# Moving the choose product from VectorE to GpSimd, and all block totals to ScalarE, in a graph network's edge ranking

## The reference, cut to what matters

```
src = concat([s, d, loop]); dst = concat([d, s, loop])      # 206250 edges, sorted by dst
x = layernorm(x + attention(x, src, dst))                    # softmax over the edges of a node
x = layernorm(x + edge_network(x, src, dst))                 # two batch norms over edges
x = layernorm(x + graph_convolution(x, src, dst))
x = layernorm(x + weighted_sum_mlp(x, src, dst, edge_weight))
```

## Time and profile before

| | us |
|---|---|
| median of 3 runs | 10757.82 (10753.19 to 10758.09) |
| the profiled execution | 10751.21 |
| its span | 10749.4 |
| VectorE busy | 8209.4 (76%) |
| TensorE busy | 8389.9 (78%) |
| ScalarE busy | 4510.4 (42%) |
| GpSimd busy | 1386.4 (13%) |

### The profile page before, as it was taken

How to read it: one execution, slowest core, us unless ns; L and a number is a source line. 1 busy time by engine, 2 the same in 40 slices (tenths; PEclk the granted TensorE clock), 3 DMA queues, 4 the chain that set the end, 5 groups by cost and what they waited for, 6 DMA issues and landing times. The chain is left out here.

```text
span 10749.4 us, 313973 instructions
## 1 busy us (share of the span) xinstructions
PE 8389.9 (78%) x96214; PEld 6815.6 (63%) x96215; DVE 8209.4 (76%) x16705; ACT 4510.4 (42%) x9074; POOL 1386.4 (13%) x1678
## 2 busy tenths in 40 slices
PE   2244668885888755899995999798999959769996
PEld 0232225664777644899994666444999936468896
DVE  4797777777999866666666999777888777788887
ACT  0120001113666411565654444586777746423333
POOL 0110001110000000466662000000000012100000
PEclk7555555556999855999997999899999979889998
DMA  2000000001444311333331888686455400000000
GB/s 49 4 0 13 4 4 11 12 12 47 162 161 161 124 36 36 109 122 125 122 125 58 273 275 274 227 291 210 143 144 145 139 12 5 4 4 3 3 3 13
DMA packets 618663, 984.99 MB, mean 92 GB/s; under 512 B 133030, under 2 KB 278381, under 8 KB 618586
## 3 DMA queue, kind: packets, MB, share of 16 engines
q1 hardware_dynamic: 487514, 810.18, 23.8%
q10 hardware_dynamic: 121152, 162.43, 4.2%
q0 software_dynamic: 9920, 11.51, 0.4%
HBM read 788.66 MB, written 195.21 MB: 92 GB/s over the span
## 5 line engine op out<-in xcount | busy, mean ns | idle before, releaser
L2523 POOL TENSOR_TENSOR acc<-acc,m_sum 128x544 f32<-128x544 f32 (+1 forms) x637 | 810.3, 1272 | 1229.4 <-ACT m_sum L2490 1189.1
L2387 DVE TENSOR_TENSOR m_msg<-m_vps,m_msg 128x512 f32<-128x512 f32 (+1 forms) x637 | 427.3, 671 | 414.5 <-PE m_vps L2428 376.7
L2452 PE MATMUL m_sps<-m_msg,m_oh 128*128 128x136 f32 x4900 | 697.9, 286 | 0.0
L2859 PE MATMUL u_sps<-u_r,u_oh 128*128 128x129 f32 x4900 | 657.0, 276 | 28.7 <-ACT u_r L2815 28.7
L1495 PE MATMUL sp_out_x<-x,sp_adj_x 128*128 128x128 f32 x4802 | 671.6, 284 | 0.0
L1479 PE MATMUL sp_aps_x<-sp_ohw_x,sp_oh_x 128*128 128x128 bf16 x7350 | 536.6, 221 | 166.5 <-DVE sp_ohw_x L1446 166.4
L2092 PE MATMUL s_qps<-q_parts,s_oht 128*128 128x128 bf16 x7203 | 511.5, 220 | 197.9 <-DVE s_oht L1562 146.3
L1508 ACT COPY sp_adj_x<-sp_aps_x 128x512 f32<-128x512 f32 (+1 forms) x637 | 362.4, 569 | 722.6 <-PE sp_aps_x L1479 722.6
L2843 PE MATMUL u_zps<-fcs,u_a 128*128 128x128 f32 x4916 | 654.7, 276 | 6.9 <-ACT u_a L2808 6.9
L2859 PEld LDWEIGHTS u_sps<-u_r,u_oh 128*128 128x128 f32 x4900 | 598.5, 192 | 37.7 <-issue 37.6
L2452 PEld LDWEIGHTS m_sps<-m_msg,m_oh 128*128 128x128 f32 x4900 | 610.5, 191 | 0.0
(11 more groups left out here) (595 smaller groups left out, 20318.6 us busy)
## 6 DMA issues: line engine op xcount, KB each, us to landing
u_e<-e_tiles SPq DMA_DIRECT2D x591, 256.0 KB, 2.8
e_tiles<-t_es ACTq DMA_DIRECT2D x588, 256.0 KB, 4.1
g_e<-e_tiles SPq DMA_DIRECT2D x588, 256.0 KB, 4.5
s_rows<-bucket_rows SPq DMA_DIRECT2D x148, 768.0 KB, 4.0
m_rows<-bucket_rows SPq DMA_DIRECT2D x148, 768.0 KB, 4.0
t_rows<-bucket_rows SPq DMA_DIRECT2D x148, 384.0 KB, 5.0
s_rows<-bucket_rows SPq DMA_DIRECT2D x49, 896.0 KB, 5.0
m_rows<-bucket_rows SPq DMA_DIRECT2D x49, 896.0 KB, 5.0
```

Source lines behind the costliest of these rows:

```text
L2452: last = nc.tensor.matmul(sps[x][:, at:at + M], oh[x][:, j * P:(j + 1) * P], msg[x][:, j * M:(j + 1) * M], start=True, stop=True)
L2523: nc.gpsimd.tensor_tensor(at, at, sums[x][:, 0:n * M], ALU.add).then_inc(added, 1)
L2859: last = nc.tensor.matmul(sps[:, :], oh[x][:, j * P:(j + 1) * P], zr[x][:, j * D1:(j + 1) * D1], start=(q == 0 and j == 0), stop=(q == las ...
```

## The change

Four things change, all inside `phase_bucket_ranks`:

- `choose` is issued by GpSimd instead of VectorE. `sel` has four buffers instead of two, with a semaphore pair for each (`chosen`, `totalled`).
- ScalarE copies the totals of all four sets, into one table; GpSimd copies none.
- The second table, its clear and the merge are gone, and SyncE waits for ScalarE's copies instead of the merge.
- `fold` waits for the previous set's second fold explicitly, which `choose` had implied.

```diff
-        sel = [sb(f"bk_sel{u}", 8 * NB1) for u in range(2)]
-        crow = [sb(f"bk_crow{e}", NB1 * NB1, F32, 1) for e in range(2)]
+        sel = [sb(f"bk_sel{u}", 8 * NB1) for u in range(R)]
+        crow = sb("bk_crow", NB1 * NB1, F32, 1)
...
-                c.go(nc.vector.memset(crow[0][:, :], 0.0))
-                c.go(nc.vector.memset(crow[1][:, :], 0.0))
+                c.go(nc.vector.memset(crow[:, :], 0.0))
...
                     dve.wait_ge(ranked[u], i)
-                    dve.wait_ge(counted[u % 2], 4 * i + u // 2 * 2 + 2)
+                    dve.wait_ge(counted, 8 * i + 2 * u + 2)
+                    dve.wait_ge(folded[(u - 1) % R], 2 * i + (2 if u else 0))
...
-                def choose(i, u):
-                    dve.wait_ge(folded[u], 2 * i + 2)
-                    nc.vector.tensor_tensor(
-                        sel[u % 2][:, :].rearrange("p (g t b) -> p g t b", g=2, t=G),
-                        ro[u][:, :].rearrange("p (g c b) -> p g c b", g=2, c=2)[:, :, 0, :].unsqueeze(2).broadcast_to([P, 2, G, NB1]),
-                        oh[u][:, :].rearrange("p (q b t) -> p q t b", q=4, t=2), ALU.mult).then_inc(chosen[u % 2], 1)
-
                 def total(i, u):
-                    dve.wait_ge(chosen[u % 2], 4 * i - 3 + 2 * (u // 2))
+                    dve.wait_ge(chosen[u], i)
...
-                    for u in range(R):
-                        fold(i, u)
+                    for u in range(R + 1):
+                        if u < R:
+                            fold(i, u)
                         if u > 0:
                             total(i, u - 1)
                             pair_hot(nc, oh[u - 1][:, :], k["iota_2"], NB1, sh[:, bass.ds(i * 32 + (u - 1) * 8, 8)], 4).then_inc(made[u - 1], 1)
-                        choose(i, u)
...
-                for e in range(2):
-                    dve.wait_ge(counted[e], 4 * n + 8)
-                nc.vector.tensor_tensor(crow[0][:, :], crow[0][:, :], crow[1][:, :], ALU.max).then_inc(merged, 1)
-                dve.wait_ge(chosen[1], n * 4)
+                for u in range(R):
+                    dve.wait_ge(totalled[u], n + 1)
...
             @block.scalar
             def _(act):
-                keep_counts(act, nc.scalar.copy, 0)
+                n = double_rounds(act, L, z)
+                act.sem_inc(counted, 16)
+                act.wait_ge(cleared, 1)
+                with act.Fori(1, n + 1) as i:
+                    for u in range(R):
+                        bs = [act.value_load(L["block"][0:1, bass.ds((i - 1) * 8 + u * 2 + g, 1)], min_val=0, max_val=s.NB) for g in range(2)]
+                        act.wait_ge(folded[u], 2 * i + 2)
+                        for g in range(2):
+                            act.wait_ge(counted, 8 * i + 8 + u * 2 + g)
+                            act.sem_inc(count_go, 1)
+                            nc.scalar.copy(crow[:, bass.ds(bs[g] * NB1, NB1)], ro[u][0:1, (2 * g + 1) * NB1:(2 * g + 2) * NB1]).then_inc(counted, 1)
 
             @block.gpsimd
             def _(pool):
-                keep_counts(pool, nc.gpsimd.tensor_copy, 1)
+                n = double_rounds(pool, L, z)
+                with pool.Fori(1, n + 1) as i:
+                    for u in range(R):
+                        pool.wait_ge(folded[u], 2 * i + 2)
+                        pool.wait_ge(totalled[u], i)
+                        nc.gpsimd.tensor_tensor(
+                            sel[u][:, :].rearrange("p (g t b) -> p g t b", g=2, t=G),
+                            ro[u][:, :].rearrange("p (g c b) -> p g c b", g=2, c=2)[:, :, 0, :].unsqueeze(2).broadcast_to([P, 2, G, NB1]),
+                            oh[u][:, :].rearrange("p (q b t) -> p q t b", q=4, t=2), ALU.mult).then_inc(chosen[u], 1)
```

More of the change, by code:

```diff
@@ L954, in phase_bucket_ranks @@
         made, ranked, folded = ([sem(f"bk_{n}{u}") for u in range(R)] for n in ("made", "ranked", "folded"))
-        counted, count_go = [sem(f"bk_counted{e}") for e in range(2)], [sem(f"bk_count_go{e}") for e in range(2)]
-        merged = sem("bk_merged")
-        chosen = [sem(f"bk_chosen{u}") for u in range(2)]
+        counted, count_go = sem("bk_counted"), sem("bk_count_go")
+        chosen, totalled = ([sem(f"bk_{n}{u}") for u in range(R)] for n in ("chosen", "totalled"))
         f5 = T["fields"][:, :].rearrange("p (g q f t) -> p g q f t", q=2, f=FQ, t=2)
@@ L978, in _ @@
                 c.go(nc.vector.tensor_copy(ones_b[:, :], k["ones"][:, :]))
-                c.go(nc.vector.memset(crow[0][:, :], 0.0))
-                c.go(nc.vector.memset(crow[1][:, :], 0.0))
+                c.go(nc.vector.memset(crow[:, :], 0.0))
                 c.step(nc.vector.memset(ro[R - 1][:, :], 0.0))
-                dve.sem_inc(cleared, 2)
+                dve.sem_inc(cleared, 1)
                 def build(i, u):
@@ L1003, in fold @@
                             op0=ALU.mult, op1=ALU.add).then_inc(folded[u], 1)
-                def choose(i, u):
-                    dve.wait_ge(folded[u], 2 * i + 2)
-                    nc.vector.tensor_tensor(
-                        sel[u % 2][:, :].rearrange("p (g t b) -> p g t b", g=2, t=G),
-                        ro[u][:, :].rearrange("p (g c b) -> p g c b", g=2, c=2)[:, :, 0, :].unsqueeze(2).broadcast_to([P, 2, G, NB1]),
-                        oh[u][:, :].rearrange("p (q b t) -> p q t b", q=4, t=2), ALU.mult).then_inc(chosen[u % 2], 1)
                 def total(i, u):
-                    dve.wait_ge(chosen[u % 2], 4 * i - 3 + 2 * (u // 2))
-                    nc.vector.tensor_reduce(rr[:, bass.ds((i - 1) * 32 + u * 8, 8)], sel[u % 2][:, :].rearrange("p (t b) -> p t b", b=NB1),
-                                            AX, ALU.add).then_inc(chosen[u % 2], 1)
+                    dve.wait_ge(chosen[u], i)
+                    nc.vector.tensor_reduce(rr[:, bass.ds((i - 1) * 32 + u * 8, 8)], sel[u][:, :].rearrange("p (t b) -> p t b", b=NB1),
+                                            AX, ALU.add).then_inc(totalled[u], 1)
                 for u in range(R):
                     dve.sem_inc(folded[u], 2)
+                    dve.sem_inc(totalled[u], 1)
                     pair_hot(nc, oh[u][:, :], k["iota_2"], NB1, sh[:, u * 8:u * 8 + 8], 4).then_inc(made[u], 1)
@@ L1039, in _ @@
                             pair_hot(nc, oh[u - 1][:, :], k["iota_2"], NB1, sh[:, bass.ds(i * 32 + (u - 1) * 8, 8)], 4).then_inc(made[u - 1], 1)
-                        choose(i, u)
-                    total(i, R - 1)
-                    pair_hot(nc, oh[R - 1][:, :], k["iota_2"], NB1, sh[:, bass.ds(i * 32 + (R - 1) * 8, 8)], 4).then_inc(made[R - 1], 1)
-                for e in range(2):
-                    dve.wait_ge(counted[e], 4 * n + 8)
-                nc.vector.tensor_tensor(crow[0][:, :], crow[0][:, :], crow[1][:, :], ALU.max).then_inc(merged, 1)
-                dve.wait_ge(chosen[1], n * 4)
+                for u in range(R):
+                    dve.wait_ge(totalled[u], n + 1)
                 c.step(nc.vector.tensor_tensor(rr[:, :], rr[:, :], pre[:, :], ALU.add))
@@ L1069, in _ @@
                         last.then_inc(ranked[u], 1)
[L1071 to L1082, removed]
@@ L1092, in _ @@
             @block.sync
             def _(sp):
-                sp.wait_ge(merged, 1)
+                n = double_rounds(sp, L, z)
+                sp.wait_ge(counted, 8 * n + 16)
                 sp.sem_inc(cleared, 1)
-                sp.dma_start(T["count"][:, :], crow[0][:, :]).then_inc(cnt_in, 16)
+                sp.dma_start(T["count"][:, :], crow[:, :]).then_inc(cnt_in, 16)
                 sp.wait_ge(cnt_in, 16)
```

## The result

| | before | after |
|---|---|---|
| median of 5 runs | 10758.1 us (10753.2 to 10760.1) | 10810.8 us (10803.1 to 10811.5) |
| ratio | | 1.0048 (1.0033 to 1.0062) |
| profiled execution | 10751.2, span 10749.4 | 10803.1, span 10801.6 |
| ranking round | 8.14 | 9.28 |
| tail starts | 816.61 | 866.19 |

What follows compares the result with a forecast made beforehand. VectorE bounds the loop before; after, ScalarE's serial chain does. Rounds of 9.26 instead of 8.14 us, less 2.6 for the clear, start the tail 49.5 later: 10808 us from the median 10757.8, range 10793 to 10850.

Steps and rivals of the forecast that it cites:

- ScalarE's round, 9.26: Ranking loop: ScalarE's table load, reads and copies for four sets take 9.26 us a round, against 8.14 now.
- The reads' cost of 1.2 us: ScalarE's queue: reading two block numbers into registers before each set's copies costs about 1.2 us, not counted as busy.
- Clear and merge, 5.3 off: VectorE's path: dropping one 2500-element clear (2.6) and the merge of count tables (2.7) gives 5.3 us.
- GpSimd's product, 1.03: Each choose product on GpSimd takes 1.03 us, from a line through f32 rows, bounded by 0.9 and 1.34.
- The handoff from fold to product, 0.20: Ranking loop: GpSimd's choose starts 0.2 us after VectorE's fold ends.
- VectorE's and GpSimd's own chain: Ranking loop: folds, GpSimd products and held one-hots alone make a round of 8.40 us, below ScalarE's 9.26.
- ScalarE keeps up, the exclusion holds: Rival in the ranking loop: some ScalarE reads run ahead or the load goes; round 8.40, +9, 10767 us; chance 0.05.
- The third rival: Ranking loop: ScalarE keeps up and GpSimd doesn't hold the one-hot; round 7.43, 44 us gained, 10714; chance 0.04.
- The exclusion of the one-hot and the product: Ranking loop: VectorE's one-hot, with both inputs in SBUF, and GpSimd's choose exclude each other; one-hots take 1 us and more.
- VectorE's waits for count copies, some 3 us a round: Ranking loop: VectorE idles some 3 us a round before a fold released by ScalarE's count copy.
- The last copy at 872.3 and the hidden store: End of ranking: ScalarE's last copy ends at 872.3, and the counts' store hides behind VectorE's tail, running to 875.7.
- "Nothing after the stage changes": Stages behind the ranking: none of them changes, so the loss is that of the ranking stage alone.

Runs made afterwards that it cites:

- e1: Changed kernel with the choose product back on VectorE and all counts still on ScalarE; 10854.0 us, ratio 1.0095.
- e3: Changed kernel without ScalarE's block-number reads, copies going to fixed places, so the counts are wrong; 10726.5 us, ratio 0.9977.
- e5: Changed kernel with a set's two block numbers packed into one word, plus fifteen one-element clears on VectorE; 10736.5 us, ratio 0.9985.
- e8: Changed kernel with two rounds in one turn of ScalarE's loop and a separate loop for a left-over round; 10769.2 us, ratio 1.0014.
- e11: Changed kernel with packed block numbers, no added one-element clears, and two 1824-column clears made one; 10723.7 us, ratio 0.9972.
- e6: Changed kernel with packed block numbers and the one-hot's number row in PSUM, plus fourteen clears; 10726.0 us, ratio 0.9973.
- e4: Changed kernel with the one-hot product reading its row of block numbers from PSUM in f32; 10822.8 us, ratio 1.0066.
- e9: Changed kernel with five one-element clears added on VectorE at the end of the ranking stage; 10853.5 us, ratio 1.0096.
- e2: Changed kernel with counts again split between ScalarE and GpSimd in two tables, choose product kept on GpSimd; 10776.9 us, ratio 1.0022.
- e10: e2 with thirteen one-element clears added on VectorE at the end of the stage; 10741.5 us, ratio 0.9990.

## Why the prediction was right, step by step

- **ScalarE's round, 9.26: right (9.28).** Its four terms came out at 1.29, 1.90, 0.43 and 1.84. Shown as the bound by e1 (the round stays without GpSimd's product), e3 and e5 (it falls to 7.66 with the reads gone or halved) and e8 (by 0.70 a round with every second load gone).
- **The reads' cost of 1.2 us: right.** It was read from queue checks and not from busy time. In after it is the 1.24 of "issue" between two sets.
- **Clear and merge, 5.3 off: consistent.** The tail starts 49.6 later; 49.5 was predicted. I didn't try either alone. That they agree to 0.1 is partly luck: the first table load starts 3.4 earlier than before and not 2.6, and 54 rounds of 9.278 are 1.0 longer than 54 of 9.26.
- **GpSimd's product, 1.03: too high.** It took 0.951 to 0.960 in all 220, between the bounds 0.9 and 1.34. The line through f32 rows doesn't quite hold for a bf16 and a broadcast input.
- **The handoff from fold to product, 0.20: too high, it is 0.08.** Together these mis-sized VectorE's and GpSimd's own chain: 8.40 predicted, 7.66 in e3. With 0.95 and 0.08 the prediction's own working gives 7.74, so they are most of the miss. It didn't matter while 9.28 lay above, but it turns a rival's sign: "ScalarE keeps up, the exclusion holds" was priced at 9 above before. The same case measured 31 below before in e11. That rival's condition didn't occur here; its price was 40 too high.
- **The third rival's sum doesn't come out.** Four sets of 1.47 with waits of 0.6 and 0.7 are 7.2, not the 7.43 that the text gives. The rows say what is missing: a round is 8.14 where four sets of 1.96 are 7.84, and these 0.3 at the turn of the round stay. With them the sum is 7.5, close to the 7.48 of e6, the run nearest to that case.
- **The exclusion of the one-hot and the product: right.** 0.86 beside a product, ended 0.23 after it, as worked out; gone with one input in PSUM (e4). Off the bound, that gives back 0.18 a round, net of the slower one-hots (e6).
- **VectorE's waits for count copies, some 3 us a round: too high**, 0.71 and 1.09 in the round shown, 91.6 us in all or 1.7 a round. The rest of the slack is there, but not as idle time: three one-hots a round are held for 0.5 each, and held time counts as busy.
- **The last copy at 872.3 and the hidden store: nearly.** The copy is at 872.20. VectorE ends its tail at 873.75+2.06 = 875.81 and the stage's end follows 2.72 later; before, it followed 2.2 later. So 0.5 us of the store may show.
- **"Nothing after the stage changes": true for after, but for a reason I hadn't seen.** It holds because the change happens to leave VectorE's fill loop at place 551. With five instructions more it would have cost 100 us (e9, against the kernel before on its chip), far outside the range given. That after stayed at 551 is luck. Of the 52.2 us between the spans 50.1 are there at the end of the fill stage; the 2 behind it lie within the spread of runs.

What stays open: which places of a loop cost what, and why; and whether the two lengths of a round account for the whole spread of e2 and e10.

## What to carry to other kernels

An engine's slack is its period less its whole chain, with the register reads, the checks, the branch and the load at the loop's top; its busy share can be a third while it sets the rate. Before work moves to such an engine, write its round from the timeline (start to start), not from its durations. And compare a stage that an edit doesn't touch before and after it: if its "issue" time moved while its instruction durations did not, the total says little about the edit. A kernel whose runs spread wider than others may have two lengths of a round: look at the single distances and not at their mean.

## What the runs showed of the hardware

- A loop on VectorE costs more or less with its place in the engine's instruction stream: 753 us at place 551 (five kernels), 766 at 552 and 567, 799 at 554 and 556, with the same durations (368 and 367 ns) and more "issue", of which a part takes the place of waits for TensorE [after and e9 above].
- A table load at the top of a loop's body recurs each turn with one function in use (the one-turn loop behind it in e8 had none), 1.28 us a record, and 1.39 are saved for each load and turn left out (e8).
- Reading two block numbers into registers on ScalarE takes 1.24 us of its queue between copies (after). With one read and two shifts the gap is 0.68 (e5).
- One PSUM input lifts the hold-up of a VectorE product beside a GpSimd product. The f32 row in PSUM costs that product 0.2 us when nothing holds it (e4: always some 0.565; 0.36 and 0.86 in after).
- When a VectorE product and a GpSimd product that exclude each other become ready within 0.05 us, either may go first, and a round takes 7.17 or 8.00 us by which does (e2: 26 and 27 rounds; e10: 6 and 47).
